# The mixer's gate product reads the projection from PSUM instead of a copy in SBUF

## What is computed

```
proj = hidden @ W_in.T            # gate (2048), hBC (2304), dt (32)
hBC  = silu(causal_conv4(hBC) + conv_b)   # -> xs (32 heads x 64), B, C
dt   = softplus(dt + dt_bias);  dA = exp(dt * A)
y_t  = state recurrence over dA, dt, xs, B, C  + D * xs
g    = y * silu(gate)             # the gate's product
g    = g * rsqrt(mean(g*g) + eps) * norm_w
out  = g @ W_out.T
```

## Time and profile before

| | us |
|---|---|
| median of 3 runs | 1433.21 (1432.12 to 1439.83) |
| the profiled execution, its own time | 1438.92 |
| its span from first to last instruction | 1437.1 |
| the mixer in it, from its first to its last instruction, about | 398 (82 to 480) |

### The profile page before, as it was taken

How to read it: one execution, slowest core, us unless ns; L and a number is a source line. 1 busy time by engine, 2 the same in 40 slices (tenths; PEclk the granted TensorE clock), 3 DMA queues, 4 the chain that set the end, 5 groups by cost and what they waited for, 6 DMA issues and landing times. The chain is left out here.

```text
span 1437.1 us, 16374 instructions
## 1 busy us (share of the span) xinstructions
PE 1207.5 (84%) x4614; PEld 642.1 (45%) x4614; DVE 887.9 (62%) x1244; ACT 599.2 (42%) x1746; POOL 552.1 (38%) x531
## 2 busy tenths in 40 slices
PE   0049889779898599999996999988799787997998
PEld 0014444334444344444443665643585346844443
DVE  7978988389985476757663635429751496504222
ACT  2026445345545232323323656647672475710110
POOL 5563675525665331313120433427651275500000
PEclk9999999999999799999998999989899898997999
DMA  6000000000003300000003000030000000000000
GB/s 254 0 22 1 0 1 1 1 0 0 0 0 121 158 0 1 0 0 0 0 33 146 1 1 0 0 139 1 1 2 1 1 0 0 0 0 8 0 0 29
DMA packets 5481, 33.24 MB, mean 23 GB/s; under 512 B 528, under 2 KB 1936, under 8 KB 3536
## 3 DMA queue, kind: packets, MB, share of 16 engines
q1 hardware_dynamic: 5424, 32.61, 5.8%
HBM read 31.56 MB, written 1.05 MB: 23 GB/s over the span
## 5 line engine op out<-in xcount | busy, mean ns | idle before, releaser
L813 POOL TENSOR_TENSOR decays<-decays,scores 128x768 f32<-128x768 f32 x64 | 124.7, 1951 | 159.3 <-ACT decays L749 159.3
L575 PE MATMUL pg<-h,weights 128*128 (+1 forms) x136 | 69.2, 634 | 85.2 <-PEq L356 82.9
L1993 POOL TENSOR_TENSOR f_pair<-m,weights 128x256 f32<-128x256 f32 x80 | 91.0, 1155 | 92.4 <-DVE m L2014 91.4
L1415 POOL TENSOR_TENSOR prob_latent<-prob_latent,inverse_latent 128x128 f32<-128x128 f32 (+1 forms) x128 | 62.1, 506 | 145.4 <-DVE inverse_latent L1405 144.9
L1106 PE MATMUL ph<-h,weights 128*128 x256 | 116.6, 600 | 0.0
L575 PE MATMUL px<-h,weights 128*128 x136 | 73.1, 663 | 30.5 <-DVE conv L886 30.4
L749 ACT ACTIVATE decays<-pcum,neg_cum 128x256 f32<-128x256 f32 (+1 forms) x256 | 87.4, 443 | 11.2 <-PE pcum L628 11.0
L1415 POOL TENSOR_TENSOR prob_gqa<-prob_gqa,inverse_gqa 128x128 f32<-128x128 f32 (+1 forms) x128 | 62.0, 506 | 58.3 <-DVE inverse_gqa L1405 56.5
L886 DVE SCALAR_TENSOR_TENSOR conv<-px,pp,conv 128x510 f32<-128x510 f32 (+2 forms) x102 | 75.1, 737 | 12.4 <-ACT conv L714 9.5
L721 ACT ACTIVATE tanh_x<-conv 128x512 f32<-128x512 f32 x36 | 22.5, 629 | 135.3 <-DVE conv L886 135.3
L1163 ACT ACTIVATE up<-ph 128x512 f32<-128x512 f32 x44 | 26.3, 597 | 124.9 <-PE ph L1106 124.7
(11 more groups left out here) (329 smaller groups left out, 3042.0 us busy)
## 6 DMA issues: line engine op xcount, KB each, us to landing
weights<-in_w_mixer SPq DMA_DIRECT2D x2, 2048.0 KB, 18.4
weights<-in_w_moe SPq DMA_DIRECT2D x2, 1536.0 KB, 7.6
moe_rest<-in_w_moe SPq DMA_DIRECT2D x2, 1536.0 KB, 13.9
weights<-in_w_gqa SPq DMA_DIRECT2D x1, 3072.0 KB, 9.9
weights<-in_w_gqa SPq DMA_DIRECT2D x1, 2048.0 KB, 14.4
weights<-in_w_moe SPq DMA_DIRECT2D x1, 1920.0 KB, 9.1
weights<-in_w_mixer SPq DMA_DIRECT2D x1, 1536.0 KB, 12.1
weights<-in_w_moe SPq DMA_DIRECT2D x1, 1152.0 KB, 11.6
```

Of the source, the lines that this page charges most:

```text
L575: op = nc.tensor.matmul(out[0:m, :], w[:, col + k * m:col + (k + 1) * m], net.h[:, ds(i * PAIR + k * TOK, TOK)], start=(k == 0), stop=(k = ...
L813: nc.gpsimd.tensor_tensor(decays[:, head % 4], decays[:, head % 4], scores[:], ALU.mult).then_inc(decay_scaled, 1)
L1415: op = nc.gpsimd.tensor_tensor(self.prob[:, slot, cols], self.prob[:, slot, cols], self.inverse[:, slot, t:t + 1].to_broadcast([P, P * (t ...
L1993: op = nc.gpsimd.tensor_tensor(out[:, :, s, :], src[:, :, 1 - s, :], sin[:, None, s, :].to_broadcast([P, 4, HALF]), ALU.mult)
```

## The change

ScalarE's copy falls away. `silu_gate` reads `pg` itself, and the waits that protected the copy's target go to DVE ahead of `silu_gate`. `gate_like(s)` for s of 1 and more waits for `gate_ready` of `silu_gate(s-1)`, instead of for the copy of step s-1; `gate_like(0)` waits for the dt product's `pg_free`.

```
     def gate_like(i, s):
         m, col = ...
-        project(pg, m, col, i, pg_free, pg_ready, i * (N + 1) + s + 1)
+        free, count = (pg_free, i + 1) if s == 0 else (gate_ready, i * N + max(s, 0))
+        project(pg, m, col, i, free, pg_ready, count)
...
     def tanh_gate(i, s):
         act.wait_ge(pg_ready, i * (N + 1) + s + 2)
         act.wait_ge(gate_ready, i * N + s)
-        if s >= 4:
-            act.wait_ge(g_ready, i * N + s - 3)
-        elif s == 0:
-            act.wait_ge(parts_ready, i + 1)
-        else:
-            act.wait_ge(pt_ready, i * (N + 2) + 1)
         nc.scalar.activation(tanh_g[:], pg[:], ACT.Tanh, scale=0.5).then_inc(tanh_g_ready, 1)
-        nc.scalar.activation(gate[:, s % 4, :], pg[:], ACT.Copy).then_inc(pg_free, 1)
...
     def softplus_cum(i, link):
-        dve.wait_ge(pg_free, i * (N + 1) + 1)
+        dve.wait_ge(pg_free, i + 1)
...
     def silu_gate(i, s):
+        if s >= 4:
+            dve.wait_ge(g_ready, i * N + s - 3)
+        elif s == 0:
+            dve.wait_ge(parts_ready, i + 1)
+        else:
+            dve.wait_ge(pt_ready, i * (N + 2) + 1)
         dve.wait_ge(tanh_g_ready, i * N + s + 1)
-        dve.wait_ge(pg_free, i * (N + 1) + s + 2)
-        v.scalar_tensor_tensor(gate[:, s % 4, :], tanh_g[:], 1.0, gate[:, s % 4, :],
-                               ALU.add, ALU.mult).then_inc(gate_ready, 1)
+        v.scalar_tensor_tensor(gate[:, s % 4, :], tanh_g[:], 1.0, pg[:], ALU.add,
+                               ALU.mult).then_inc(gate_ready, 1)
```

## The result

The changed kernel took 1486.8 us (median of 4 runs, 1482.07 to 1496.22) against 1433.4 of the kernel before: 1.037 times as long, 95% interval 1.031 to 1.044. That is 53 us more, where 11.8 had been forecast, and outside the range. The direction and the place were right, the size was not. One execution of a later run, the first with the product ahead of y, was in a slower state of the chip (1870 us at a granted clock of 0.66): the median given there counts it, the ratio does not.

The account below looks back on a forecast made before the run. In the mixer DVE sets the pace in steps 4 to 10, PE nearly in 11 to 14. +7.0 - 0.4 - 0.7 = +5.9 us a pair, +11.8 for both: 1445 us on the 1433.21 median; range 1422 to 1460.

Parts of the forecast that it names:

- The copy is worth nothing, ACT waits anyway: ACT in the mixer: dropping 32 copies, 18.8 us, counted 0, since ACT waits 55.1 us for DVE's taps.
- The product costs 0.06 us more: silu_gate on DVE, one PSUM input: 746 ns against 682 undisturbed, +0.06 us a step, not added separately.
- The new wait closes a loop of 6.93 + x: Mixer steps: no step shorter than 6.93 us plus x, 10.25 undisturbed, 11.9 to 12.4 stretched.
- x between 3.32 and 5.46 by whether POOL stretches g and `silu_x`: DVE's time from y's start to silu_gate's end: 3.32 us undisturbed, 4.96 to 5.46 stretched.
- `pg` start to the end of `mix`: 6.85 us: PE's part of the loop: 6.85 us, 6.93 with an estimated 0.08 for two semaphores.
- The clock: Rival, chance 0.15: PE idling in each step falls to its lower clock in most late steps; about +36 us, 1469.
- Steps 4 to 10 hardly change (-0.4): Mixer steps 4 to 10: DVE nearly always busy, loop only clips short steps; 78.4 us against 78.7 a pair.
- Steps 11 to 14 at 47.6: Mixer steps 11 to 14: four steps at 11.9 us, 47.6 against 40.6, +7.0 a pair.
- The end of a pair (-0.7): After silu_gate(14): loop adds 0.7 us, PE's higher clock may return up to 2.9; taken as -0.7 a pair.

Follow-up runs that it names:

- the product ahead of y: Changed kernel with silu_gate moved ahead of y on DVE and the gate's tanh ahead of the convolution's on ACT: 1418.1 us, ratio 0.985; run again, 1417.1 us.
- the order alone: Kernel before, copy and SBUF product kept, with silu_gate ahead of y and gate's tanh and copy ahead of the convolution's tanh: 1424.5 us; run again, 1420.3 us.
- the wait alone: Kernel before, copy and SBUF product kept; only the gate projection's wait changed, to the previous step's product: 1506.4 us, ratio 1.049.
- POOL cut: POOL's decay scaling and sum of squares cut to 8 columns: 1440.5 us in the changed kernel, 1400.1 us in the kernel before.

## Why the prediction was wrong

- *The copy is worth nothing, ACT waits anyway*: right in the whole time. ACT's waits for the taps stayed, and with the order alone and the copy kept the kernel is as fast as without it, within 3 us. By place it is not nothing, as said above: the 5 us behind the mixer were in no term of the sum.
- *The product costs 0.06 us more*: wrong, and small. Its 32 instances last 669 to 681 ns, no more than the undisturbed SBUF product. It is never stretched, as predicted. The Trainium skill (SBUF — State Buffer, Who interferes with whom) says that a DVE instruction with at most one SBUF input, outside the 2-port modes, does not contend with GpSimd; the trace agrees, 681 ns at most.
- *The new wait closes a loop of 6.93 + x*: right in kind, shown by the wait alone (slow), by the product ahead of y (fast) and by POOL cut (10.21 us a step).
- *x between 3.32 and 5.46 by whether POOL stretches g and `silu_x`*: right in the mean, 4.64, where the sum had used about 4.5; single steps went up to 6.44.
- *`pg` start to the end of `mix`: 6.85 us*. This is the step that failed. I took it as a constant from one row of a stretch at the full clock. With 8.13 instead of 6.93 in 22 steps it made 22 x 1.20 = 26.4 us, of which 1.8 are the wait for the exponentials in step 4 of each pair and the rest stands in the 14 steps whose matmuls were slow. At 6.93 and the measured x the 22 steps would have taken 22 x 11.57 = 254.5 against 236.5, +18 us; the sum had +13.2 for them. The clock was among the rivals, with a chance of 0.15 and at about 1 us in late steps only, some 4 us a pair where it came to about 12; so even that rival ended at 1469 us. Its estimate of PE's work in a step, 9.1 us, does not follow from its rows: 42.6 / 45.0 of 10.15 is 9.6. I had seen that idling cost PE its clock and that the loop makes PE idle in every step, and did not put the two together in the sum.
- *Steps 4 to 10 hardly change (-0.4)*: wrong, and mostly for the same reason. In the first pair they took 90.9 us, not 78.4; at 6.93 and the x measured there it would have been 82.0. That y would wait little there was wrong as well: it waited 0.9 to 5.0 us in each step. *Steps 11 to 14 at 47.6*: measured 46.9 in the first pair, right by luck: two errors, a shorter x (3.9) and two steps at the lower clock, cancel.
- *The end of a pair (-0.7)*: from the end of `silu_gate(14)` to the last y +0.2 us in the first pair and +4.4 in the second, where the product's end of step 14 to the next y took 8.6 us, and the next gap was longer too.

The rest of the 53 us is not settled to the microsecond: by the profiled execution 47.0 are in the mixer and 5 behind it, with the cause of these open, and the kernel's runs differ by 14.

## What to carry to other kernels

When a buffer's release moves from one engine's early copy to a later instruction of another, follow what stands ahead of that instruction back to the engine that waits: if it leads to that engine's own last result, a pipeline of several steps has become a loop, and the sum of its parts is the new step. Price the parts of such a loop at the clock that PE will have while it idles in it, not at the clock of a row taken when PE was busy throughout. Where the release is late, move the instruction ahead of what it need not wait for; that alone was worth 1% here.

## What the hardware showed that I had not expected

- More work on PE made the kernel faster: two products that add zero in each step, some 1.7 us, raised the granted clock from 0.91 to 1.00 in about steps 4 to 10 and took 17 to 25 us off.
- DVE's product with one PSUM operand lasts 672 ns in the median against 682 with two SBUF operands, while y, also with one PSUM operand, lasts 748. So the operand's place is not what sets y apart; what does was not tried.
- The time that DVE instructions are stretched by does not simply go when one of them escapes. In the changed kernel the product is never stretched, and its 32 instances take 9.9 us less; but g and `silu_x` take 15.9 us more in all, `silu_x` up to 2839 ns for one:

```profile
L889 DVE SCALAR_TENSOR_TENSOR xs<-tanh_x,conv x32: 679/693/2839, 108.6 to 499.4; 128x512 f32<-128x512 f32 x32
...
L900 DVE SCALAR_TENSOR_TENSOR gate<-tanh_g,pg x32: 669/672/681, 109.3 to 502.2; 128x512 f32<-128x512 f32 x32
...
L934 DVE SCALAR_TENSOR_TENSOR y<-xs,pp,py x32: 737/748/749, 127.9 to 520.5; 128x512 f32<-128x512 f32 x32
```
